# The attention loop's GpSimd order: the second norm's inverse root ahead of the row stores and the masked values

## The reference, cut to what matters

```python
def _layernorm(x, w, b):
    m = jnp.mean(x, axis=-1, keepdims=True)
    v = jnp.mean(jnp.square(x - m), axis=-1, keepdims=True)
    return (x - m) * jax.lax.rsqrt(v + EPS) * w + b
...
x = x + _msa(_layernorm(x, ln1_w, ln1_b), w_qkv, w_proj)
x = x + _moe_mlp(_layernorm(x, ln2_w, ln2_b), gate_w, gate_b, w1, w2)
```

## Time and profile before

| what | value |
|---|---|
| time, median of 3 runs | 514.15 us (514.02 to 514.8) |
| span of the profiled execution, first to last instruction | 510.8 us |
| around the span, by the median | 3.35 us |
| PE busy | 473.7 us (93%) |
| DVE (VectorE) busy | 353.8 us (69%) |
| ACT (ScalarE) busy | 324.2 us (63%) |
| POOL (GpSimd) busy | 241.7 us (47%) |
| granted TensorE clock, mean | 0.989 of full speed |

### The profile page before, as it was taken

The page is one execution under the profiler, slowest core; times in us unless marked ns, Lnnn a source line. Parts: engine busy times, 40 slices in busy tenths (PEclk is TensorE's granted clock), DMA queues, the critical chain, the costliest instruction groups (busy, mean ns, idle before and its releaser), DMA issues. The chain is left out here.

```text
span 510.8 us, 24000 instructions
## 1 busy us (share of the span) xinstructions
PE 473.7 (93%) x9062; PEld 391.8 (77%) x9062; DVE 353.8 (69%) x1264; ACT 324.2 (63%) x809; POOL 241.7 (47%) x580
## 2 busy tenths in 40 slices
PE   3899999999999999999999998789999989999992
PEld 3689999999986635666666677678888878999991
DVE  5778888888878685767657655568888887645440
ACT  4655555555546864656666567578777778977770
POOL 3644444444445001055443545724677756776552
PEclk9899999999999999999999999999999999999996
DMA  9262000000000066143223000710111116365210
GB/s 249 89 205 86 0 0 0 0 0 0 0 1 1 2 137 151 51 84 84 82 60 112 3 0 2 277 56 4 36 58 47 48 48 187 125 165 151 62 35 10
DMA packets 24221, 34.60 MB, mean 68 GB/s; under 512 B 3632, under 2 KB 17973, under 8 KB 23768
## 3 DMA queue, kind: packets, MB, share of 16 engines
q1 hardware_dynamic: 21376, 27.23, 19.3%
q0 software_dynamic: 2784, 6.56, 3.6%
HBM read 25.98 MB, written 8.26 MB: 67 GB/s over the span
## 5 line engine op out<-in xcount | busy, mean ns | idle before, releaser
L223 ACT ACTIVATE den_v<-ps_g,floor 128x128 f32<-128x128 f32 x124 | 45.3, 367 | 43.8 <-PE ps_g L254 39.6
L268 PE MATMUL ps_g<-buf_b,v_pad 128*32 128x128 f32 x1984 | 67.2, 277 | 0.2 <-issue 0.2
L254 PE MATMUL ps_g<-buf_a,u_pad 128*32 128x128 f32 x1984 | 66.3, 274 | 0.1
L254 PEld LDWEIGHTS ps_g<-buf_a,u_pad 128*32 128x32 f32 x1984 | 53.2, 111 | 0.4 <-DVE u_pad L340 0.3
L268 PEld LDWEIGHTS ps_g<-buf_b,v_pad 128*32 128x32 f32 x1984 | 51.1, 111 | 1.0 <-issue 0.4
L1406 POOL DMA_INDIRECT out<-buf_d,token_i x39 | 38.8, 996 | 23.3 <-DVE buf_c L1909 16.6
L748 PE MATMUL ps_h<-buf_c,up 128*128 128x512 f32 x96 | 49.1, 607 | 0.6 <-DVE buf_c L1027 0.4
L362 DVE RECIPROCAL v_pad<-ps_g 128x32 f32<-128x32 f32 x124 | 38.7, 333 | 14.6 <-PE ps_g L260 12.3
L205 POOL TENSOR_SCALAR held_u<-inv_u 128x8 f32<-128x8 f32 x124 | 24.5, 197 | 39.4 <-DVE inv_u L371 38.7
L1394 POOL DMA_INDIRECT sorted_x<-rows,slot_i x32 | 32.4, 1011 | 20.3 <-DVE slot_i L1850 13.1
L1618 PE MATMUL ps_ss<-xT,buf_d 128*128 128x128 f32 x312 | 41.4, 276 | 0.5 <-ACT xT L1744 0.2
(11 more groups left out here) (370 smaller groups left out, 1238.7 us busy)
## 6 DMA issues: line engine op xcount, KB each, us to landing
cw_b<-cw_d SPq DMA_DIRECT2D x16, 512.0 KB, 7.9
buf_c<-sorted_x SPq DMA_DIRECT2D x39, 136.0 KB, 2.4
buf_b<-in_x_t SPq DMA_DIRECT2D x4, 512.0 KB, 6.2
buf_d<-in_x_nt SPq DMA_DIRECT2D x1, 2048.0 KB, 9.6
x<-in_w SPq DMA_DIRECT2D x1, 2048.0 KB, 8.9
buf_b<-in_w SPq DMA_DIRECT2D x1, 2048.0 KB, 13.2
buf_a<-in_x SPq DMA_DIRECT2D x3, 512.0 KB, 5.5
sorted_x<-nobody SPq DMA_DIRECT2D x1, 1088.0 KB, 12.0
```

The lines of the kernel that those rows point to most:

```text
L223: fn(den_v[:, h, :], ps_v[h], ACT.Relu, bias=floor[:]).then_inc(v_den, 1)
L254: last = mm(ps_v[h][32 * j:32 * j + 32, :], u_pad[:, h, j, 32 * i:32 * i + 32], K[:, t * D:(t + 1) * D], start=i == 0, stop=i == TI - 1)
L268: last = mm(ps_u[h][32 * c:32 * c + 32, :], v_pad[:, h, c, 32 * i:32 * i + 32], KT[:, b * N:(b + BG) * N], start=i == 0, stop=i == TI - 1)
```

## The change

In chunks 4, 6, ... 14 GpSimd's `inverse_root` goes from the end of its list for the chunk to the front, before the wait for the scores, the two row stores and the masked values.

```diff
                 for c in range(NC):
+                    if c >= 4 and c % 2 == 0:
+                        inverse_root(c // 2 - 2)
                     placed = sum(2 * S.SIZES[n] for n in range(GROUPS) if S.last[n] + 5 <= c)
                     if sent < placed:
                         pool.wait_ge(s_mm, c + 1)
...
                         sent = t + 1
                     if c + 1 < NC:
                         place_values(c + 1)
-                    if c >= 4 and c % 2 == 0:
-                        inverse_root(c // 2 - 2)
                 pool.wait_ge(o_mm, NC - 1)
```

## The result

The changed kernel takes 516.65 us (median of six runs, 515.4 to 517.38), the kernel before 513.43 in the runs beside it (six, 512.06 to 514.8). The ratio is 1.0059, 95% interval 1.004 to 1.0078: about 3 us slower, where 1.7 was forecast. The profiled execution of it took 516.65 us, and its span is 514.9.

What follows compares the result with a forecast made beforehand. The attention loop was taken as bound by a chain through GpSimd's list, with VectorE's `choose` waiting for the root. 0.10 + 1.17 + 0.45 = 1.72 us takes 514.15 to 515.9 us, range 515.0 to 516.9 (513.3 to 517.2 with the shorter hold).

Steps and rivals of the forecast that it cites:

- The root: GpSimd, even chunks: the inverse root is made about 3.96 us after `most`, almost four us earlier than before.
- The queue behind it: GpSimd's two stores and `vb` follow the root; `vb` ends 1.56 us later, which costs its reader `mix` nothing.
- The hold: VectorE's `choose`: `vb` holds `logits` until 0.15 us before `vb` ends, so it ends 0.39 us later per turn.
- The turns: Attention loop, chunks 8, 10, 12: each turn 12.47 us instead of 12.08, 3 x 0.39 = 1.17 us.
- chunk 6: First turn affected: `logits` ends +0.15 us later, or about -0.05 if VectorE arrives early; taken as +0.10 us.
- The faster mixes: Mixes without a store beside them take 0.77 us instead of 1.00; the forecast had them bring nothing.
- Chunk 14: Behind the loop: `vb` holds VectorE's tables 1.03 us; 0.62 is taken up by a wait, +0.45 us taken.
- The 3.35 us around the span: Time outside the profiled span, untouched by the change; added to a span of 512.5 to give 515.9 us.
- Short instructions do not pass beside `vb`: Rival denied here: `choose`'s short instructions pass beside `vb`, `rank`'s waits go; 511 us, chance 0.16.
- the hold is not shorter: Rival denied here: `vb` finishes reading about half-way, turns within 0.4 us of before; 513.5 to 514.6, chance 0.16.
- GpSimd was not the bound: Rival denied here: slower stores make GpSimd's list the bound, `vb` 1.2 us later each turn; 520 us, chance 0.03.
- rival C: Rival in the follow-ups: the stretch of low clock was chance, with the excess near +1.7 us instead of +3.

Runs made afterwards that it cites:

- the second profile: The changed kernel, unaltered, run and profiled again: ratio 1.0046 to the kernel before, stretch 67.17 us, no low clock.
- the three faster kernels: Changed kernel with `vb` between the two stores, ahead of both, or ahead of both with `over_sum` of chunk 14 before the tables: 0.995, 0.9925, 0.9935 of before.
- the tail filled: Changed kernel with extra matmuls in `rank` and between the two halves of chunk 15's transposes, where TensorE waits: ratio 1.0045 to the kernel before.

## Why the prediction was right, and where it was not

**The time.** Forecast were 515.9 us, 1.72 more than before; measured 516.65. That the two lie so near is in part luck: the kernel before came out at 513.43 us in the runs beside it, not 514.15, so the change cost about 3 us (2.4 in the second set of runs). The direction and the hold were right, and the sum was too small.

**The root.** Forecast 3.96 us after `most`, measured 3.90. **The queue behind it.** `vb` forecast 7.55 us after `most`, measured 7.49; `mix` didn't suffer. All of it went as the rows had it.

**The hold.** `logits` forecast to end 9.49 us after `most`, 0.04 us behind `vb`; measured 9.45 to 9.46 in the turns from chunk 8 on, and everywhere 0.05 to 0.06 behind `vb`. The row of a far larger pair of products carried over to a 0.18 us instruction unchanged. The Trainium skill, SBUF — State Buffer, section "Who interferes with whom", would have VectorE's whole instruction behind GpSimd's, `vb`'s end plus 0.18; by its usual 0.18 us the runs let it start about 0.12 us before that end, near the 0.15 of the row. By the same section of the Trainium skill an instruction with at most one SBUF input passes; `most`, which reads PSUM, does (1.21 us beside `vb`, above).

**The turns.** 12.47 forecast; 12.42 to 12.44 measured where the clock stayed up. Three turns cost 1.04 us in the second profile (1.17 forecast), chunk 6 +0.08 (+0.10). The faster mixes (0.77 us nearly everywhere) brought nothing: `rank` waited the longer.

**Chunk 14, the term that was mis-sized.** Forecast +0.45, measured +0.95 without low clock. The failed step is "the wait of 0.62 us before the last `over_sum` takes up most": by the waits of the second profile, that wait was no slack. It is a wait for the last `mix`, which stands behind transposes that wait for the `over_sum` of chunk 14, which stands behind the held table instruction. The wait moves with the hold; after it, it is still 0.61 us. With the 1.03 us left whole the sum would have been 2.3, and the profile with a full clock shows 2.07.

**What the forecast lacked.** Low clock. In the first profile it took the place of the hold behind chunk 14 (L1878 took 0.16 us there) and cost more than it: 67.83 - 67.17 = 0.66 us net over the second profile. That makes 2.7 of the 3.0 us of the ratio.

**Beside the point.** The 3.35 us around the span were half of that: in every run since, the time stands 1.67 to 1.77 us above the span. The profiled execution of the kernel before was thus about 1.6 us under the first median (510.8 + 1.72 against 514.15). It shifts no term, since the difference was added to the median.

**The rivals.** Short instructions do not pass beside `vb`, and the hold is not shorter: `logits` ended 0.05 to 0.06 us behind `vb` in all eight places of the two profiles of the changed kernel. GpSimd was not the bound; it becomes that with 2 us more a turn, and then at 12.9 us, by way of another hold.

## What to carry to other kernels

Moving a late producer forward isn't enough: look at what moves back behind it, and which of the other engine's instructions it then lies beside. Here the same early root costs 0.5% with `vb` last and gains 0.75% with `vb` in front of the stores, where VectorE reads PSUM. And a wait at the end of a chain is slack only if what it waits for doesn't hang on the delayed work itself.

## What was not expected of the hardware

TensorE's granted clock fell to 0.50, its 1.2 GHz level, seven times between chunk 6 and 440 us in six of the nine profiles of kernels slower than before, each time over two or three neighbouring windows of 2 us, and never in the five of the kernel before and of faster ones. Right ahead of each fall TensorE had waited 0.99 to 1.67 us for VectorE, in `rank` or at another place. But ten waits of 1.00 to 1.60 us in the same profiles went by without one. In the five, and with the tail filled, where no fall came either, it waited 0.91 us at most from chunk 6 on.

Chance alone (rival C) does not explain the falls. The mean granted clock over all executions was 0.9909 in 64 of the kernel before and 0.9910 in 23 of the three faster kernels, but 0.9884 in the 13 of the changed kernel and 0.9878 in the 74 of all slower ones, it among them (single executions: 0.979 to 0.995). Low clock goes with the slower orders; which execution meets it is another matter. The Trainium skill, TensorE: Matmul & The Clock Gate, Part 1, has the clock follow how busy the array has been and the moment of a change vary from run to run; the profiles agree with that, but no run here forces or prevents a fall, so that what decides it stays open.

A fall costs less than it seems: a turn that it slows by 0.5 us (12.93 against 12.42) brings VectorE to `logits` after `vb` has ended, and then nothing is held (in the kernel with chunk 14 as before, `logits` of chunk 9 took 0.18 us).

Held time is shown as an instruction's own duration and as its engine's busy time, and as nobody's wait: 1.63 us for an instruction of 0.18.
